# One table load ahead of everything on ScalarE, in a decoder layer with attention, retention and experts

## The reference

```python
def _layernorm(x, axis=-1, eps=1e-05):
    m = jnp.mean(x, axis=axis, keepdims=True)
    v = jnp.var(x, axis=axis, keepdims=True)
    return (x - m) / jnp.sqrt(v + eps)
...
    x = _layernorm(x + _L0_attn_ref(x, L0_attn_Wq, L0_attn_Wk, L0_attn_Wv, L0_attn_Wo, L0_attn_bo), axis=-1)
    x = _layernorm(x + _L0_xattn_ref(x, ctx_1024, ctx_1024), axis=-1)
    x = _layernorm(x + _L0_ffn_ref(x, L0_ffn_gate, L0_ffn_experts_w1, L0_ffn_experts_w2, L0_ffn_experts_w3), axis=-1)
```

## Time and profile before

| | |
|---|---|
| median of 3 runs | 1083.97 us (1081.84 to 1084.67) |
| profiled execution | 1086.72 us, span 1084.9 us |
| granted TensorE clock over the span | 0.854 of full speed |
| busy: PE, DVE, ACT, POOL | 838.3, 766.1, 804.6, 579.6 us |

### The profile page before, as it was taken

The page is one execution under the profiler, slowest core; times in us unless marked ns, Lnnn a source line. Parts: engine busy times, 40 slices in busy tenths (PEclk is TensorE's granted clock), DMA queues, the critical chain, the costliest instruction groups (busy, mean ns, idle before and its releaser), DMA issues.

```text
span 1084.9 us, 34400 instructions
## 1 busy us (share of the span) xinstructions
PE 838.3 (77%) x11844; PEld 611.1 (56%) x11844; DVE 766.1 (71%) x2039; ACT 804.6 (74%) x1672; POOL 579.6 (53%) x567
## 2 busy tenths in 40 slices
PE   2677888878787878888877657179999999999700
PEld 2455555545454554545444333169999999999600
DVE  5888776767676767777764433558888888888665
ACT  1234789999999999999999996456666666666445
POOL 0367664767676767677675222514444444444443
PEclk8778999888888888989886765589999999999955
DMA  7411222121211212121112100312222222222177
GB/s 223 128 23 33 39 39 41 29 59 31 61 32 48 43 49 43 47 46 40 38 38 44 45 21 18 82 50 61 66 63 63 62 61 66 63 63 61 38 230 237
DMA packets 136742, 68.50 MB, mean 63 GB/s; under 512 B 74528, under 2 KB 125984, under 8 KB 136576
## 3 DMA queue, kind: packets, MB, share of 16 engines
q1 hardware_dynamic: 121440, 40.56, 16.2%
q0 software_dynamic: 8640, 17.84, 5.0%
q10 hardware_dynamic: 6496, 7.89, 2.3%
HBM read 37.91 MB, written 28.34 MB: 61 GB/s over the span
## 4 chain that ended last, share of the span: by engine, by line
PE 63%; issue 10%; ACT 5%; POOL 3%; DVE 2%; DMA 1%; SPq 0%; POOLq 0%; ACTq 0%; DVEq 0%
PE QKV L780 9%; PE ST L780 8%; PE ST L652 8%; PE YY L599 6%; PE XT L808 5%; PE SC L572 5%; PE SC L808 5%; PE ST L667 3%; PE QKV L558 3%; PE YY L695 2%; POOL frs L1614 1%; PE TR L617 1%; PE ST L678 1%; ACT L895 1%; PE XT L543 1%
## 5 line engine op out<-in xcount | busy, mean ns | idle before, releaser
L1560 POOL TENSOR_TENSOR prod_ev<-e_sb,q_v 128x512 f32<-128x512 f32 x256 | 296.0, 1193 | 169.2 <-ACT e_sb L870 143.3
L1601 POOL DMA_INDIRECT token_halves<-w_new,tok_i x142 | 136.2, 959 | 191.2 <-DVE w_new L1503 169.3
L1576 POOL DMA_INDIRECT routed_rows<-xe,pos x128 | 124.4, 972 | 111.9 <-DVE pos L1340 84.8
L1170 DVE TENSOR_TENSOR prod_qk<-q_v,QKV 128x2048 f32<-128x2048 f32 x64 | 145.8, 2280 | 21.9 <-PE SC L572 19.7
L652 PE MATMUL ST<-q,k_t 64*64 64x512 f32 x512 | 96.5, 831 | 69.9 <-issue 48.3
L1050 ACT CAST prod_ev<-prod_qk 128x1024 f16<-128x1024 f32 x71 | 74.2, 1045 | 73.5 <-DVE prod_qk L1513 53.0
L1487 DVE TENSOR_TENSOR prod_ev<-prod_qk,prod_ev 128x1024 f16<-128x1024 f32 x71 | 87.0, 1226 | 56.2 <-ACT prod_ev L1050 56.2
L780 PE MATMUL QKV<-k_t,w_hl 128*128 128x256 f16 x852 | 116.9, 274 | 0.0
L780 PE MATMUL ST<-k_t,w_hl 128*128 128x256 f16 x852 | 116.8, 273 | 0.0
L599 PE MATMUL YY<-prod_ev,tab 128*32 128x144 f32 x2048 | 87.0, 318 | 25.4 <-issue 20.7
L1059 ACT ACTIVATE prod_qk<-QKV,silu_scale 128x512 f32<-128x512 f32 x142 | 96.2, 678 | 10.7 <-PE QKV L780 7.7
(11 more groups left out here) (171 smaller groups left out, 1758.6 us busy)
## 6 DMA issues: line engine op xcount, KB each, us to landing
w_new<-routed_rows SPq DMA_DIRECT2D x71, 130.0 KB, 2.2
prod_ev<-token_halves SPq DMA_DIRECT2D x16, 512.0 KB, 5.2
x_sb<-x SPq DMA_DIRECT2D x128, 32.0 KB
head_rows<-o_n SPq DMA_DIRECT2D x128, 32.0 KB
o_t<-head_rows SPq DMA_DIRECT2D x64, 64.0 KB, 2.5
ctx_sb<-ctx SPq DMA_DIRECT2D x32, 128.0 KB, 2.4
out<-prod_qk ACTq DMA_DIRECT2D x16, 256.0 KB, 4.4
token_halves<-w_new,tok_i POOLq DMA_INDIRECT x142, 2.2
```

The costliest lines, as they stand in the source:

```text
L1170: eng.tensor_tensor(prod_qk[:, u, :, :].rearrange("p d (i j) -> p d i j", j=NH), q.unsqueeze(3).to_broadcast([P, HD, NH, NH]), k.unsqueeze ...
L1560: ins = eng.tensor_tensor(prod_ev[:, u, q, :, :, 0:HD], e_sb[:, it.slot(2), u, 64 * q:64 * q + 64].rearrange("p (i j) -> p j i", j=4).unsq ...
L1576: eng.indirect_dma_start(out=xs, out_offset=bass.IndirectOffsetOnAxis(ap=pos[:, r, 2 * u + k:2 * u + k + 1], axis=0), in_=xe[:, r, u, k, : ...
L1601: eng.indirect_dma_start(out=halves, out_offset=bass.IndirectOffsetOnAxis(ap=tok_i[:, s, u:u + 1], axis=0), in_=yw[:, s, u, :], in_offset= ...
```

## The change

```diff
@@ -822,6 +822,7 @@
 
         @block.scalar
         def _(eng):
+            eng.add_instruction(mybir.InstLoadActFuncSet(name=nc.get_next_instruction_name(), act_func_set_id=6, engine=mybir.EngineType.Activation))
             eng.wait_ge(x_in[0], 64)
             eng.dma_start(fresh(0).rearrange("p (e i) -> p e i", e=n_exp), w1.rearrange("e h i -> h e i")).then_inc(w_in[0], 16)
```

## The result

The changed kernel takes 951.18 us (median of 3, 946.74 to 953.46) against 1083.97 us: a ratio of 0.8772, 95% interval 0.8718 to 0.8826. The forecast was 974 us in a range of 951 to 1014. Direction and mechanism came out; the gain is 133 us where 110 were forecast: the median lies at the range's lower end, the ratio just past it (0.8772 x 1083.97 = 950.9). Kernels with four loads per duo (the kernel before, e1, e10) have single executions of 1055 to 1072 us among many near 1081, so for e1, e10 and e12, whose ratios these shift, medians of all executions are given alone.

A forecast was written before the change was run, and what follows sets the result against it. ScalarE's table loads were taken to keep TensorE waiting in the first part; gains of 75.4 (steps 19 to 40), 30 (after) and 4.7 us (before) sum to 110, giving 974 us from 1083.97, range 951 to 1014.

The forecast's parts named there:

- Loads go: ScalarE: with a table holding both functions active from the start, 129 loads go and only Silu's remains besides the new one.
- the first rival: ScalarE's loads stay: the hand-written load is not counted, 130 follow it, and the time is 1084 us; 8%.
- Both gaps: TensorE's waits for ScalarE before L599 and L652, 0.86 and 2.14 us in a step, were to close.
- The step that failed: Steps 19 to 40: 18.39 us each falls to 14.8, gaining 75.4 us, bounds 51 and 90.
- The floor itself: Steps 19 to 40: GpSimd's products and scatters keep a step from falling below 14.1 to 14.4 us.
- The running-down steps: Seven steps from 563.78 us: six gain 4.0 us each, 24 together, and the seventh, with two loads, 2.7 us.
- The end: Behind 674.60 us: four more loads go, but GpSimd's scatters become the bound; gain 3.5 us.
- The start: Steps before 177.50 us: gain 4.7 us together, bounds 0 and 9.
- Rival two, the heads' trip: Heads' round trip through HBM sets steps 19 to 40 at 16.3 us, total 1008 us, counted from 990 up; 17%.
- Rival three, the clock: TensorE's granted clock stays at 0.68 in steps 19 to 40: 20.6 us per step, 1095 us in all; 3%.

The follow-up runs named there:

- e1: Changed kernel with redundant loads of the same table put back at all four places of each duo; 1081.24 us.
- e10: Kernel before, with its loads, and SP's load of the heads put ahead of the loads of x; 1077.07 us.
- e12: Changed kernel with heads loaded first and half of one of GpSimd's eight products per duo given to VectorE; 932.04 us.
- e2: Changed kernel with only the three loads per duo between L949 and L921 put back; 1080.85 us.
- e3: Changed kernel with only the load before the first norm's logarithm put back, 32 in all; 951.71 us.
- e8: Changed kernel with one load per duo put back, ahead of the gate's exponential; 967.83 us.
- e9: Changed kernel with two loads per duo put back, at the first norm's and the gate's exponentials; 1007.96 us.
- e4: Changed kernel with SP's load of the heads put ahead of the loads of x and of the context; 939.34 us.
- e11: Changed kernel with heads loaded first and one of GpSimd's eight products per duo given to VectorE; 935.89 us.

## Why the prediction was right or wrong

**Loads go, the first rival falls.** Two loads are left, as forecast, and the table that was loaded is counted as active: no load stands at L856, which runs at 12.26 us, where the kernel before has one at its L855.

**Both gaps close.** They did; e2 brings them back with three loads and e3 shows the fourth to be free. My reading that ScalarE was "the fullest engine" was true and beside the point: not its 17.2 us of work in 18.39 set the step but a loop, TensorE over L949 and ScalarE's work up to L921 back to TensorE. In the step of the earlier trace rows the loop closes: TensorE from L652 at 406.68 us to the end of L667 at 416.87, ScalarE from L949 at 416.94 to the end of L921 at 424.53, L652 again at 424.63. TensorE's timeline of the kernel before has the row that is needed for it:

```profile
415.79 1.08 PE L667 MATMUL ST<-sm,ctx_bd 128*32 128x128 f32 x32
```

**The step that failed** is the size of the new step: "I take 14.8, near TensorE's and GpSimd's sums, with a little for engines that can't all meet". By L949 it is 13.96 us; 21 x 0.84 = 17.6 us of the 25.6 by which the profiled gain, 135.6 us, passes the 110. The floor itself, "14.1 to 14.4 us" for GpSimd, held (the 14.39 us read from the earlier trace rows had some 0.3 us of waiting for VectorE's positions in it): from 192.40 to 475.42 us GpSimd goes through twenty cycles of 14.00 to 14.35 us, in the mean 14.15, without a wait over 0.4 us. GpSimd's timeline after, the products of steps 19, 20 and 40:

```profile
178.10 9.15 POOL L1561 TENSOR_TENSOR prod_ev<-e_sb,q_v 128x512 f32<-128x512 f32 x8 [4.79 <-ACT e_sb L871]
...
192.40 9.04 POOL L1561 TENSOR_TENSOR prod_ev<-e_sb,q_v 128x512 f32<-128x512 f32 x8
...
475.42 9.02 POOL L1561 TENSOR_TENSOR prod_ev<-e_sb,q_v 128x512 f32<-128x512 f32 x8
```

What failed is what I put on top of the floor. First, TensorE's sum: I took 14.3 to 14.96 us, from rows with a granted clock of 0.88 (14.3 is 14.96 less the 0.68 us between L652's 1.70 and 1.02 us in the earlier trace rows). At 1.00 it is 95.48 us in 100 (200 to 300 us, after), 13.3 us per step. Second, the engines do meet: three of them are 92 to 95% busy at once, and nothing has to be added to the fullest one's cycle. That L949's step is another 0.2 us shorter than this cycle is no lower floor, since TensorE gets ahead of GpSimd: the products start 5.25 us behind L950 in step 19 (172.85 us) and 9.34 us behind it in step 40 (466.08 us), and the step from 478.88 to 496.04 us takes 17.16 us: in it VectorE's L1333 is held up for 5.99 us, until GpSimd's products end at 484.44 us, and L652 waits 3.48 us for VectorE.

**The running-down steps** brought 33.0 us for 24 + 2.7. The loads there were sized about right, the clock was put at nothing. Before, in the step from 636.69 us, TensorE takes 8.43 us from L652 to the end of L667, and ScalarE 6.46 us from L949 to the end of L921; after, in the step from 518.73 us, they take 6.36 and 2.22 us. So ScalarE's part falls by 4.24 us, where I said 4.0, and TensorE's by 2.07 us, where I said nothing. Three of the seven steps are like this; the three ahead of them gain 9.2 us together, where I said 12, as one of them is the step of 17.16 us. TensorE's timeline before and then after (L652 takes 1.09 us there instead of 1.99):

```profile
636.69 1.99 PE L652 MATMUL ST<-q,k_t 64*64 64x512 f32 x8 [4.08 <-ACT k_t L921]
...
644.04 1.08 PE L667 MATMUL ST<-sm,ctx_bd 128*32 128x128 f32 x32 [1.44 <-DVE sm L1255]
```

```profile
518.73 1.09 PE L652 MATMUL ST<-q,k_t 64*64 64x512 f32 x8 [0.42 <-ACT k_t L922]
...
524.01 1.08 PE L667 MATMUL ST<-sm,ctx_bd 128*32 128x128 f32 x32 [1.44 <-DVE sm L1256]
```

The granted clock is 0.50 in the first of these four (636.7 to 638.6 us) and 1.00 in the stretch of the last two (518.7 to 525.0 us). In the kernel before it is 1.00 from 418.5 to 423.0 us and 0.50 from 424.6 to 427.6 us, behind L652's gap of 2.14 us in the earlier trace rows. That TensorE's clock is the cause is read from these rows and from e2, e8 and e9; no run changed the clock alone.

**The end** (4.9 us for 3.5) came as said: GpSimd's scatters run from 548.93 us without a break over 1 us to the end of the first part, and little more could be had there.

```profile
548.93 0.96 POOL L1577 DMA_INDIRECT routed_rows<-xe,pos  x1 [1.40 <-DVE pos L1341]
...
568.40 0.95 POOL L1577 DMA_INDIRECT routed_rows<-xe,pos  x1 [0.31 <-issue]
```

**The start** (4.7 us for 4.7) hit by luck in good part: e1, with all four loads of a duo, comes to step 19 at 171.68 us and e2 at 174.25 us, where the changed kernel has 172.85 and the kernel before 177.50. Profiles of kernels with the same loads differ there by more than the gain that I put down to the loads. e4, which comes to step 19 at 162.24 us, shows that the heads' trip held the steps there.

**Rival two, the heads' trip,** was the next bound up to step 24, but at 13.7 to 15.6 us and not at 16.3. **Rival three, the clock,** went the other way: it rose, from 0.86 to 1.00 at 200 to 400 us.

## What to carry to other kernels

Here TensorE's work got shorter when its waits closed (the same instructions took 10.6 us with three loads, at a granted clock of 0.87 in the stretch, and 8.7 us with one, at 1.00), so take TensorE's new sum at the clock that its rows show where it isn't waiting. What a load (or any instruction) costs is read from the loop that it lies in, not from its engine's share: here one of four equal loads cost nothing and the third of the others almost twice what the second did. The next bound's floor, read as the fullest engine's cycle less the waits in it that the change closes, held here (14.1 forecast, 14.15 measured); a margin for engines that can't all meet was not needed. Check the second bound too: with GpSimd lightened the heads' trip held the step at 13.67 us, half a microsecond below GpSimd's cycle.

## What the runs showed of the hardware

Two instructions of VectorE, L1333 and e11's L1256, were held up while GpSimd ran its products. In the changed kernel L1333 takes 0.17 to 0.20 us where it runs between the products of one duo and the next, and 0.41 to 1.63 us in the four steps from 427 to 470 us, where it meets them. In e4 it meets them in nearly every step: in the step shown it takes 1.47 us (mean 1.458 in thirteen steps, once 5.96 us, 0.175 in the kernel before) and ends at 332.26 us; GpSimd's products end at 329.92 + 2.29 = 332.21 us. VectorE's row of e4 and GpSimd's:

```profile
330.79 1.47 DVE L1333 TENSOR_TENSOR posw<-oh,posf 128x32 f32<-128x32 f32 x1
```

```profile
329.92 2.29 POOL L1561 TENSOR_TENSOR prod_ev<-e_sb,q_v 128x512 f32<-128x512 f32 x2
```

A busy VectorE (199.65 us of 200 in e4) is then partly a waiting one. What it is that holds these instructions up no row shows. L1333 is not let in between two products: it ends some 0.05 us after the last of the eight each time, while e11's L1256 is through 1.5 us after the first of seven has started.
